# The last query projection of an attention turn moved to the end of its step, and the remainders of both query projections moved behind the row maxima

## The reference

```python
x = x + 0.5 * ffn(layernorm(x), w_gate, w_up, w_down)
x = x + attn(layernorm(x), W1, b1, W2, b2, Wg, bg, Wo, bo)
x = x + 0.5 * ffn(layernorm(x), w_gate, w_up, w_down)

# attn: 16 heads of 64, window 64
h = silu(x @ W1.T + b1) @ W2.T + b2
q, k, v = split(h @ Wg.T + bg, 3)
dots = einsum('bhid,bhjd->bhij', q, k) * 64 ** -0.5
dots = where(j >= i + 64, -inf, dots)          # a row sees the columns up to i + 63
out = einsum('bhij,bhjd->bhid', softmax(dots), v)
return out @ Wo.T + bo
```

## Time and profile before

| | |
|---|---|
| median of three runs | 1319.61 us (1318.7 to 1322.14) |
| the profiled execution | 1320.83 us |
| span of its records | 1319.1 us |
| granted TensorE clock, mean | 0.994 of full speed |
| PE busy | 1264.3 us (96%) |
| POOL busy | 1152.6 us (87%) |
| DVE busy | 936.3 us (71%) |
| ACT busy | 846.4 us (64%) |

### The profile page before, as it was taken

One profiled execution on the slowest core, in us unless ns is written; L12 is line 12 of the kernel. 1 busy time (PEld: TensorE's weight loads), 2 busy tenths in 40 slices (PEclk: granted clock), 3 DMA queues, 4 the chain that ended last, 5 costly groups with the idle time before them and its releaser, 6 DMA issues.

```text
span 1319.1 us, 35416 instructions
## 1 busy us (share of the span) xinstructions
PE 1264.3 (96%) x11374; PEld 1003.1 (76%) x11374; DVE 936.3 (71%) x2126; ACT 846.4 (64%) x1898; POOL 1152.6 (87%) x1086
## 2 busy tenths in 40 slices
PE   6988999999999999999999999999999999999988
PEld 5856777777777777877777777777777777777777
DVE  6856777777677777777677777777776776777755
ACT  3655666666666666666666666666666667666642
POOL 6838999999999999999999999999999999999983
PEclk9997999999999999999999999999999999999999
DMA  4242112111121121121111122121111111220001
GB/s 138 85 152 98 43 50 65 65 46 58 65 65 65 65 65 56 34 65 65 56 49 65 65 65 65 65 65 30 60 65 65 41 63 65 65 65 7 8 17 49
DMA packets 80962, 80.22 MB, mean 61 GB/s; under 512 B 38049, under 2 KB 65314, under 8 KB 80930
## 3 DMA queue, kind: packets, MB, share of 16 engines
q1 hardware_dynamic: 80930, 79.82, 18.7%
HBM read 47.13 MB, written 8.39 MB: 42 GB/s over the span
## 4 chain that ended last, share of the span: by engine, by line
PE 68%; issue 13%; DVE 9%; ACT 5%; POOL 1%; SPq 1%; DMA 1%; DVEq 1%; ACTq 0%; POOLq 0%
PE banks L995 18%; PE banks L1012 15%; PE banks L973 15%; PE banks L899 5%; DVE negmax L739 5%; PE banks L953 3%; PE banks L864 3%; PE banks L1017 3%; ACT probs L546 3%; DVE banks L734 2%; PE banks L894 2%; ACT qt L468 2%; PE banks L856 1%; PE banks L857 1%; POOL probs L449 1%
## 5 line engine op out<-in xcount | busy, mean ns | idle before, releaser
L449 POOL TENSOR_SCALAR probs<-probs,recips 128x256 f32<-128x256 f32 (+7 forms) x512 | 881.8, 1725 | 105.9 <-DVE recips L744 105.8
L554 ACT ACTIVATE probst<-banks 128x512 f32<-128x512 f32 (+2 forms) x512 | 266.0, 545 | 276.6 <-PE banks L995 276.6
L546 ACT ACTIVATE probs<-banks,negmax 128x320 f32<-128x320 f32 (+7 forms) x512 | 399.8, 788 | 65.1 <-DVE negmax L739 56.1
L739 DVE TENSOR_REDUCE negmax<-banks 128x1 f32<-128x320 f32 (+7 forms) x512 | 393.9, 811 | 31.9 <-PE banks L973 4.0
L995 PE MATMUL banks<-ident,probs 128*128 128x128 f32 x2304 | 331.2, 280 | 2.0 <-DVE probst L751 1.3
L973 PE MATMUL banks<-kt,qt 64*128 64x512 f32 (+4 forms) x2496 | 303.1, 369 | 29.1 <-ACT probs L546 29.1
L995 PEld LDWEIGHTS banks<-ident,probs 128*128 128x128 f32 x2304 | 250.4, 141 | 82.4 <-issue 74.3
L1012 PE MATMUL banks<-probst,vs 128*64 128x128 f32 (+1 forms) x3328 | 278.2, 317 | 0.1
L973 PEld LDWEIGHTS banks<-kt,qt 64*128 64x128 f32 x2496 | 192.1, 186 | 92.3 <-ACT probs L546 49.1
L1012 PEld LDWEIGHTS banks<-probst,vs 128*64 128x64 f32 x3328 | 201.4, 137 | 72.0 <-issue 22.3
L451 POOL TENSOR_SCALAR ends<-probs,recips 128x64 f32<-128x64 f32 x448 | 198.7, 443 | 0.0
(11 more groups left out here) (72 smaller groups left out, 1040.0 us busy)
## 6 DMA issues: line engine op xcount, KB each, us to landing
xth<-h_split SPq DMA_DIRECT2D x62, 512.0 KB, 4.1
hslot<-h_sb SPq DMA_DIRECT2D x32, 512.0 KB, 3.1
wsplit<-w_split SPq DMA_DIRECT2D x31, 256.0 KB, 4.5
vh<-vs SPq DMA_DIRECT2D x64, 112.0 KB, 2.3
h_split<-qt SPq DMA_DIRECT2D x16, 256.0 KB, 2.2
wslot<-in_wqkvt SPq DMA_DIRECT2D x32, 64.0 KB, 2.5
w_split<-kt SPq DMA_DIRECT2D x4, 512.0 KB, 4.2
y<-xres SPq DMA_DIRECT2D x8, 256.0 KB, 2.3
```

The lines of the kernel that those rows point to most:

```text
L449: last = nc.gpsimd.tensor_scalar(here, here, recips[:, c, h:h + 1], None, ALU.mult)
L546: nc.scalar.activation(probs[c][:, h, :], src, ACT.Exp, bias=negmax[:, c, h:h + 1], accum_out=sums[:, c, h:h + 1]).then_inc(exped.sem, 1)
L554: nc.scalar.activation(probst[c // 2 % 2][:, 4 * g:4 * g + w, c % 2 * P:(c % 2 + 1) * P], banks[:, TRANSPOSED[g % 2], 0:w * P].rearrange(" ...
L739: nc.vector.tensor_reduce(negmax[:, c, h:h + 1], rows[:, h, 0:hi], AX.X, ALU.max, negate=True).then_inc(maxed.sem, 1)
```

## The change

PE: in step 6 the projection of q1 is no longer issued behind the first two groups of transposes but last, behind the output projection and the groups 2 and 3 (`AT_END = {6}`). ACT: the high part of q1 moves with it, from before group 3's take to the first place of step 7. DVE: the remainder of q0 moves from the end of step 5 to behind step 6's maxima, and that of q1 from the end of step 6 to behind step 7's maxima (`REST_LATER`). `REST_FIRST` is empty and adds nothing. The waits are the same as before, each with its instruction. In the last turn, which projects nothing, nothing changes.

```diff
+    AT_END = {6}
+
+    REST_FIRST = ()
+    REST_LATER = ("q0", "q1")
 ...
         # ACT, step
+                def high(job):
+
+                    if job[0] in "kq" and runs(job, carry, more):
+                        queries_keys(job, job_turn(job, i), 1 - r if job_turn(job, 0) else r)
+
+                if c - 1 in AT_END:
+                    high(JOBS[c - 1])
                 for g in mine:
                     if g < 2:
                         take(tc, g, ti)
...
-                job = JOBS.get(c, "none")
-                if job[0] in "kq" and runs(job, carry, more):
-                    queries_keys(job, job_turn(job, i), 1 - r if job_turn(job, 0) else r)
+                if c not in AT_END:
+                    high(JOBS.get(c, "none"))
...
         # DVE, step
+                rest = JOBS.get(c - 1, "none")
+                if rest in REST_FIRST:
+                    evict(rest, i, r, carry, more)
                 row_max(c, i)
+                if rest in REST_LATER:
+                    evict(rest, i, r, carry, more)
...
-                if job[0] in "kq":
+                if job[0] in "kq" and job not in REST_FIRST + REST_LATER:
                     evict(job, i, r, carry, more)
...
         # PE, step
+                given = c in JOBS and runs(job, carry, more)
+                score(c, i, r)
+                if turning:
+                    turns_of(tc, ti, (0, 1))
+                if given and c not in AT_END:
+                    run_job()
                 if turning and attending:
                     turns_of(tc, ti, (2, 3))
...
                 if turning and not attending:
                     turns_of(tc, ti, (2, 3))
+                if given and c in AT_END:
+                    run_job()
```

More of the change, by code:

```diff
@@ L1030, in step, with run_job @@
                 attending = c in ATTEND_AT and (carry or c >= PV_LAG)
-                score(c, i, r)
-                if turning:
-                    turns_of(tc, ti, (0, 1))
                 job = JOBS.get(c, "none")
-                if c in JOBS and runs(job, carry, more):
+                def run_job():
                     k = JOB_ORDER.index(job)
```

## The result

The change makes the kernel slower by a little under half a percent. The median is 1326.19 us (1325.5 to 1327.05, 6 runs) against 1319.15 us (1318.25 to 1322.82, 6 runs) of the kernel before on the same chips, a ratio of 1.0045 with a 95% interval from 1.0034 to 1.0055. The time lies inside the range given, near its upper end: it is the case called rival 2, not the forecast. The loss of 7.0 us by the medians is a hair more than the range allowed over its own starting point (1326.5 - 1319.61 = 6.9 us). The profiled execution of the change took 1326.61 us with a span of 1324.8 us, 5.7 us more than the span before.

The account below looks back on a forecast made before the run. PE was taken as the bound, with a 0.48 us wait ahead of score(7) exchanged for 0.51 us ahead of q1. 31 turns times +0.05 us gave +1.6 us on 1319.61 us: 1321.2 us, range 1314.0 to 1326.5 us.

Parts of the forecast that it names:

- rival 2: q1's first matmul waits longer for q0's remainder, or restarts dearer: up to 0.21 us a turn, 1326.1 us, chance 0.24.
- What bounds the kernel: PE 96% busy; the 0.48 us wait ahead of score(7) for step 6's exponentials is all the change can win.
- DVE and ACT in step 6: Mask starts 0.06 us behind score(6), 0.42 us sooner; ACT passes on 0.22 us of it to the exponentials.
- The new wait: On PE in step 6, q1 waits for q0's remainder, starting at 632.92 us after 0.51 us idle.
- What q1 then takes: From q1's start to score(7): 0.70 to 0.79 us, so score(7) 0.02 to 0.11 us late, taken as 0.05 us.
- the lower value: q1 takes 0.70 us, its length without overlap with its neighbours, putting score(7) 0.02 us late.
- the upper bound: q1 takes 0.79 us plus 0.10 us for restarting after a wait, putting score(7) 0.21 us late.
- One wait of 0.48 us for one of 0.51 us: On PE, the wait ahead of score(7) is exchanged for one ahead of q1; score(7) 0.02 to 0.11 us later.
- Step 7: Maxima come 0.4 us sooner with q1's remainder behind them; nobody on the path wants it, so worth 0.
- forecast of no difference: Whole kernel: +0.05 us a turn, 1.6 us in all, 1321.2 us; chance 0.63.
- My own sign of being wrong: Among the signs listed: a turn that differs from 36.16 us by more than 0.13 us.
- The most that could be won: Score(7) 0.22 us sooner with the exponentials, 31 turns: 6.8 us; ACT's takes prevent more.

Follow-up runs that it names:

- e9: The kernel before, with only ACT writing q0's high part ahead of copying the attention's result in step 5: 1312.27 us, ratio 0.9943.
- e1: The change, but q1 is projected in the middle of step 6 as before; both remainders stay behind the maxima: 1368.29 us, ratio 1.0373.
- e2: The change, but q0's remainder is back at the end of step 5, ahead of the mask: 1319.66 us, ratio 1.0006.
- e5: The change with q0's remainder back in step 5 and q0's high part ahead of the attention copy; q1 still last: 1313.95 us, ratio 0.9954.
- e3: The kernel before with only q1's remainder moved behind step 7's maxima: 1318.39 us, ratio 0.9990.
- e6: The kernel before with q0's high part ahead of the attention copy and q1's remainder behind step 7's maxima: 1312.96 us, ratio 0.9949.
- e4: The kernel before with only q1's projection moved last in step 6, both remainders in their old places: 1329.36 us, ratio 1.0078.
- e10: e9 with q0 projected between the two groups of transposes of step 5 instead of behind both: 1313.04 us, ratio 0.9940.

## Why the prediction came out as it did

**What bounds the kernel: right.** 0.48 us ahead of score(7) was the place, and the chain over q0's high part, remainder, mask, maxima and exponentials was the cause; e9 moves only the high part, and score(7) comes 4.50 us after score(6) instead of 4.73 us.

**DVE and ACT in step 6: right, to the hundredth.** The mask was to come 0.06 us behind score(6) and came 632.12 - (630.75 + 1.30) = 0.07 us behind. The exponentials were to gain 0.22 us: the first one starts 633.64 - 630.75 = 2.89 us after score(6), before it was 631.99 - 628.87 = 3.12 us, so 0.23 us.

**The new wait: right.** q1 was to start 632.92 - 628.87 = 4.05 us after score(6); it starts 4.06 us after.

**What q1 then takes: the step that was mis-sized.** I priced q1 between 0.70 us, its length without the overlap with its neighbours, and 0.79 us, its spacing to output o0, and took 0.75 us or so; it is 0.89 us to score(7). The reason given for staying near the lower value, that score(7) no longer restarts from idle, bought nothing. Both values come from one row in which the successor is another one: 0.79 us was the distance to a matmul with a full 128x128 tile, whose weights are loaded under q1's last matmul. Only the upper bound had the right size (0.79 + 0.10 us), and for a wrong reason: I put the 0.10 us on the restart after a wait, but e1 has the same restart and 0.80 us. A pair of rows with the right kind of successor stands in the trace of before, in PE's timeline of step 5, q0's projection and attend with its 128x64 tile, 0.86 us on:

```profile
625.68 0.94 PE L899 MATMUL banks<-xth,wsplit 128*128 128x512 f32 x3
626.54 2.18 PE L1012 MATMUL banks<-probst,vs 128*64 128x256 f32 x32
```

With it score(7) would have been forecast 0.18 us late, 5.6 us in all, and rival 2 would have been the likeliest case.

The idle time ahead of q1 was smaller than forecast, 0.44 us and not 0.51 us, for another reason: without q1 between them the transposes and o0 take 0.07 us more than I subtracted (PE was through 3.61 us after score(6) where I had 3.54 us). It made no difference to score(7), as PE waited then anyway. It is the 0.07 us that e2 and e5 show. "One wait of 0.48 us for one of 0.51 us" was also no measure of the change: the measured idle time fell by 0.04 us, and the turn grew by 0.23 us.

**Step 7: half right.** The maxima came sooner (637.03 - 635.70 = 1.33 us behind score(7), before 1.84 us) and nobody wanted it (e3, e9 and e6). But it isn't worthless within the change: with q1 projected late and its remainder ahead of the mask, score(0) waits 0.32 us (e4). I had said that score(0) followed PE's work without a wait, and had not worked out what the change would cost with only this part left away.

**The chances.** The forecast of no difference had 0.63 and rested on a cost of 0.05 us a turn with 0.13 us as the border; a term that I had only between 0.02 and 0.21 us was then taken near its lower end. The mechanism was the forecast's, the size rival 2's. My own sign of being wrong came true: the turn differs from 36.16 us by 0.23 us, and the border was 0.13 us. That the time still lies inside the range is luck to that extent: its upper end rests on a bound with the wrong reason, and the kernel before was 0.46 us faster this time than the 1319.61 us that the range starts from.

**The most that could be won.** I had put it at 6.8 us. e9 gains 7.9 us by the medians, and 6.5 and 8.3 us by the spans of its two profiled executions; score(7) came 0.23 us sooner, 7.1 us in 31 turns. The size of the bound was right within that scatter.

## What to carry to other kernels

A wait that is hidden isn't gone: before an operation is moved into a gap, ask what it waits for itself, and whether the same change moves that further back; here q1 went into the gap ahead of score(7) and its releaser went behind the maxima, so a gap of 0.48 us was refilled by one of 0.44 us. Compare starts and not idle times: the second gap was the shorter one and held PE up by 0.69 us. When a chain runs over several engines, look for its idle stretch on the other side: DVE and ACT were both idle before score(6) ended, and one instruction of ACT one place sooner won 0.5% where the whole change lost 0.45%. Price a moved group of matmuls by a row in which it stands ahead of the same kind of successor.

## What the runs showed of the hardware

A projection of three matmuls of 512 columns takes 0.78 to 0.80 us from its start to the next matmul if that has a full 128x128 tile, whether PE had waited ahead of it (e1, 0.80 us) or not (e10, 0.78 us), and 0.86 to 0.89 us if that has a tile of 64 rows or 64 columns (before 0.86 us, the change and e9 0.89 us). In the latter case the next weight load comes 0.36 us after the projection's last load has ended. The same holds for the attention's other seams in the trace of before, by the medians: a load of the same full shape that needn't wait for its input starts within 0.01 us of the start of the matmul ahead of it. Where the shape changes between full and half it starts 0.20 us after a matmul of 128 columns, with a semaphore wait on the load or without, and 0.31 to 0.32 us after one of 512 (projection to attend, score to transposes). Why is not settled. In e10, putting transposes between saved nothing.

The Trainium skill ("TensorE: Matmul & The Clock Gate", on the queue depths) says that weight loads can be pulled ahead of matmuls in flight. Behind this projection they were, but only where the next load had the same tile shape.

Where PE's work runs on without a wait, the record of a projection starts up to 0.25 us before the recorded end of the matmul ahead of it (e2). The recorded ends of matmuls are modelled, so neither that overlap nor the idle time behind a wait is exact; the starts are what these sums go by.
